# Choice 1's first tiles start inside choice 0's last pass, and the expert bias is weighed ahead of the product

## The chip, the cores and the metric

The kernel runs on one core of a Trainium2 chip. The metric is the device time of one execution in microseconds (us), here the median of several runs; smaller is better. One more execution is recorded by the hardware profiler, and every row below is from it. PE is the matrix engine (TensorE), DVE the vector engine, ACT the scalar engine, POOL is GpSimd, and SP only issues DMAs.

## What is computed

The block takes x (4 x 2048 tokens of 512 numbers), adds a gated cross attention over 77 context tokens, and then a gated mixture of experts. Only the second part matters here. It is, shortened:

```python
gate_probs = softmax(layernorm(x) @ gate_w.T + gate_b)     # 8 experts and 2 that do nothing
weights, selected = top_k(gate_probs, 2)
norm_w = weights * (selected < 8) / their_sum
out = sum over the two choices of norm_w * (y @ expert_w[e] + expert_b[e])   # y = layernorm(x)
x = x + tanh(g_ffn) * out
```

So each token goes through the expert of its choice 0 and then through that of its choice 1.

## The kernel before

**The whole.** `fold_context` prepares weights, `attend` makes the attention of all 64 tiles of 128 tokens and the routing, and `run_experts` does the experts. Each function is a block of its own, with a meeting of all engines between them. The first two take 1009 us of the 1440 and are almost untouched; the experts take the rest.

**The table.** For every token and choice `attend` writes a row (token, weight, layernorm numbers) into a table in HBM, sorted by expert, with scatters that POOL issues (`scatter`, L1544, 128 rows each). The weight already has the factor tanh(g_ffn). The last group's scatters for choice 1 are left for the start of `run_experts`. There SP fetches the slots of the table, pass by pass, once the scatters have landed.

**The tiles of the experts.** Choice 0 has 50 tiles of 128 tokens here, choice 1 has 70. They are worked off in passes of five (R = RING = 5): a first pass written out, a loop `Fori` with a conditional body for the inner passes (the longest possible count, so that some turns are skipped), and a last pass written out. The helper `run` makes these for every engine. At the start of each pass DVE and PE load the five expert numbers into registers (L1679). A tile goes this way:

1. DVE names its tokens (`name_token`, L1877); POOL gathers its rows (L1740) into a ring of five. For choice 0 a row is x alone (256 KB a tile), for choice 1 it is x and the sum so far, as choice 0 left it (512 KB).
2. ACT normalizes it to y (L1845); PE transposes y (L1799); ACT makes the high half of the transposed y (`high_y`, L1837), DVE the low half (`low_y`, L1890).
3. PE multiplies (`multiply`, L1812, 12 matmuls) into one of three banks.
4. DVE's `finish`: it adds the bias to product / W_SCALE into `biased` (L1894), names the target rows (L1907 or L1910), and makes result = biased * weight + what was gathered (L1914).
5. POOL scatters the result: for choice 0 into the sum in `comb`, for choice 1 into the output (both L1761).

**What sets the order.** Every engine works through a list that is written out by hand. At step s PE has transpose s+1, then product s; DVE has low half s+1, `finish` of s, token names of s+5; POOL has the scatter of s-1, then the gather of s+4, which goes into the ring place that result s-1 has just freed. Semaphores carry all waits.

**Between the choices.** Choice 1 adds to sums which choice 0 writes, so a full gather has to wait until all scatters of choice 0 have landed. Four tiles (EARLY = 4) are therefore split: their x half is gathered during choice 0's last pass, their sum half afterwards. PE, ACT and DVE begin choice 1 only behind choice 0, ACT and DVE with a wait for all of its tiles.

## Time and profile before

| what | us |
|---|---|
| median of 3 runs | 1445.18 (1445.16 to 1447.43) |
| the profiled execution | 1441.85 |
| its span, first to last instruction | 1440.1 |
| first product of choice 0 | 1023.4 |
| first product of choice 1 | 1191.1 |
| end of the last product | 1432.3 |

PE is busy 1311.1 us of the span (91%), DVE 1139.6 (79%), ACT 794.6 (55%), POOL 694.6 (48%). A busy share over the whole says little of the last 430 us; read it by stages. [...] A timeline row has the start, the duration, the engine, the line and what is written from what; in square brackets stands how long the engine had been idle and what ended this. Buffers of `run_experts` are lent from `m_sb`, and the expert bias lies in `u_sb`, so those names stand in the rows.

### The profile page before, as it was taken

What the parts mean: (1) busy time and instruction counts of PE and PEld (TensorE: products, weight loads), DVE (VectorE), ACT (ScalarE), POOL (GpSimd) and SP (SyncE); (2) the same over time, 40 slices, a digit from 0 to 9 for tenths busy, and PEclk for the clock granted to TensorE, in tenths of its full rate; (3) what the DMA queues carried; (4) which work ended last, traced back from release to release, by engine and by line L of the source; (5) the groups of instructions that cost most, each with busy time, mean ns of one, the idle gap of its engine ahead of it and who ended that gap; (6) DMA issues with size and microseconds to landing.
All of it is one profiled execution on the core that took longest, in us unless ns stands there. A gap on an engine that the chain in (4) does not pass through costs nothing. (4 is left out here: it accounts for less than half of the span.)

```text
span 1440.1 us, 31728 instructions
## 1 busy us (share of the span) xinstructions
PE 1311.1 (91%) x7185; PEld 675.0 (47%) x7186; DVE 1139.6 (79%) x2910; ACT 794.6 (55%) x2838; POOL 694.6 (48%) x648
## 2 busy tenths in 40 slices
PE   5576699999999999999999999995699987999997
PEld 3432255555555555555555555552355543444443
DVE  5876688899999999999999999987466664666655
ACT  5775666666666666666666566661444433444432
POOL 0370123344554554454454545446566656566664
PEclk9896899999999999999999999997799998999999
DMA  5895578889897798987798987775355535677772
GB/s 195 207 270 167 171 159 198 193 208 238 222 215 188 184 225 197 252 204 191 186 233 206 247 192 188 183 167 159 95 153 152 157 126 171 201 242 223 233 224 91
DMA packets 434736, 277.64 MB, mean 193 GB/s; under 512 B 340478, under 2 KB 368190, under 8 KB 434543
## 3 DMA queue, kind: packets, MB, share of 16 engines
q1 hardware_dynamic: 406830, 202.76, 58.3%
q0 software_dynamic: 27840, 74.18, 16.3%
q8 instruction: 22, 0.36, 0.1%
q14 instruction: 44, 0.35, 0.1%
HBM read 121.27 MB, written 82.58 MB: 142 GB/s over the span
## 5 line engine op out<-in xcount | busy, mean ns | idle before, releaser
L857 PE MATMUL scores<-m_sb,zT 128*128 (+2 forms) x2304 | 415.6, 339 | 8.6 <-PEq L156 8.6
L972 ACT ACTIVATE expd<-scores,less 128x77 f32<-128x77 f32 x1024 | 317.4, 328 | 185.4 <-DVE less L1074 184.4
L872 PE MATMUL mix<-u_sb,pT 128*128 128x512 f16 x1728 | 383.5, 379 | 1.1 <-DVE x_out L1099 1.1
L1812 PE MATMUL out_bank<-w_parts,m_sb 128*128 x1440 | 338.8, 386 | 4.9 <-issue 4.1
L857 PEld LDWEIGHTS scores<-m_sb,zT 128*128 128x128 f16 x2304 | 220.8, 98 | 176.0 <-issue 12.0
L872 PEld LDWEIGHTS mix<-u_sb,pT 128*128 128x128 f16 x1728 | 169.0, 98 | 198.2 <-DVE x_out L1099 1.3
L1812 PEld LDWEIGHTS out_bank<-w_parts,m_sb 128*128 128x128 f16 x1440 | 143.2, 99 | 156.9 <-issue 19.9
L972 ACT ACTIVATION_READ_ACCUMULATOR expd<-scores,less 128x1 f32 x1024 | 213.5, 209 | 0.0
L1544 POOL DMA_INDIRECT table<-payload,row_i x128 | 158.9, 1241 | 59.5 <-issue 38.1
L1441 POOL TENSOR_TENSOR z_parts<-z,z_parts 128x512 f16<-128x512 f32 x62 | 71.7, 1156 | 193.2 <-ACT z_parts L963 193.2
L1894 DVE SCALAR_TENSOR_TENSOR m_sb<-out_bank,u_sb 128x512 f32<-128x512 f32 x120 | 82.8, 690 | 97.8 <-PE out_bank L1812 97.6
L1837 ACT CAST m_sb<-yT_bank 128x512 f16<-128x512 f32 x120 | 70.2, 585 | 153.1 <-PE yT_bank L1799 153.1
L1446 POOL TENSOR_TENSOR x_moments<-x_spread,minus_half 128x1 f32<-128x1 f32 x64 | 65.3, 1021 | 132.3 <-DVE x_spread L1109 132.3
L1890 DVE TENSOR_TENSOR m_sb<-yT_bank,m_sb 128x512 f16<-128x512 f32 x120 | 82.0, 684 | 44.8 <-issue 22.9
L1072 DVE TENSOR_REDUCE top<-scores 128x5 f32<-128x385 f32 (+1 forms) x192 | 111.1, 579 | 4.8 <-PE scores L857 4.7
L1799 PE MATMUL yT_bank<-ident,m_sb 128*128 128x128 f32 x480 | 76.6, 284 | 40.9 <-ACT m_sb L1845 36.9
L1761 POOL DMA_INDIRECT out_dram<-m_sb,token_out x70 | 72.7, 1038 | 76.5 <-DVE token L1877 42.2
L1845 ACT ACTIVATE m_sb<-two_ring,slots 128x512 f32<-128x512 f32 x70 | 56.9, 813 | 70.4 <-DMA two_ring<-comb,token 65.0
L1082 DVE SCALAR_TENSOR_TENSOR expd<-expd,inverse 128x1232 f32<-128x1232 f32 x64 | 92.3, 1442 | 2.2
L1799 PEld LDWEIGHTS yT_bank<-ident,m_sb 128*128 128x128 f32 x480 | 57.6, 144 | 76.1 <-ACT m_sb L1845 57.9
L1090 DVE TENSOR_TENSOR p_parts<-expd,p_parts 128x1232 f16<-128x1232 f32 x64 | 91.8, 1434 | 0.0
L1740 POOL DMA_INDIRECT two_ring<-comb,token x66 | 68.4, 1037 | 20.1 <-issue 20.1
(177 smaller groups left out, 1738.8 us busy)
## 6 DMA issues: line engine op xcount, KB each, us to landing
comb<-x_out SPq DMA_DIRECT2D x64, 512.0 KB, 3.2
x_ln<-in_x_dram SPq DMA_DIRECT2D x64, 256.0 KB
x_res<-in_x_dram SPq DMA_DIRECT2D x64, 256.0 KB, 2.8
w_raw<-in_L_ffn_expert_w_dram SPq DMA_DIRECT2D x64, 128.0 KB, 2.3
m_dram<-m_stage SPq DMA_DIRECT2D x32, 231.0 KB, 4.5
u_dram<-m_sb SPq DMA_DIRECT2D x48, 154.0 KB
m_sb<-m_dram SPq DMA_DIRECT2D x12, 616.0 KB, 4.5
u_sb<-u_dram SPq DMA_DIRECT2D x6, 1024.0 KB, 6.8
```

Source lines behind the costliest of these rows:

```text
L857: last = pe.matmul(scores[s][k][:, 0:n], zT[:, s, zp, t, :], m, start=(t == 0 and (zp, mp) == PRODUCTS[0]), stop=(t == DT - 1 and (zp, mp) ...
L872: last = pe.matmul(mix[:], pT[:, s, pp, k, :], u_sb[:, k, up, :], start=(k == 0 and (pp, up) == PRODUCTS[0]), stop=False)
L972: last = act.activation(expd[:, s, h * KEYS:(h + 1) * KEYS], scores[s][k][:, at:at + KEYS], ACT.Exp, bias=less[:, s, h:h + 1], scale=1.0 / ...
L1072: dve.tensor_reduce(top[:, s, h0:h0 + nh], bank, AX_X, ALU.max).then_inc(top_ready, 1)
L1082: dve.scalar_tensor_tensor(e, e, P_SCALE, inverse[:, s].unsqueeze(2).broadcast_to([P, HEADS, KEYS]), ALU.mult, ALU.mult).then_inc(p_ready, 1)
L1090: dve.tensor_tensor(p_parts[:, 1, 0:COLS], expd[:, s, :], p_parts[:, 0, 0:COLS], ALU.subtract).then_inc(p_lo_ready, 1)
L1544: pool.indirect_dma_start(table, bass.IndirectOffsetOnAxis(ap=self.row_i[:, side, TOP_K * t + k:TOP_K * t + k + 1], axis=0), self.payload[ ...
L1761: pool.indirect_dma_start(to, bass.IndirectOffsetOnAxis(ap=c.token_out[:, s, :], axis=0), result[:, s, :], None, bounds_check=to.shape[0] - 1,
L1799: last = pe.transpose(c.yT_bank[s][:, t, :], y[:, s, t * P:(t + 1) * P], ident[:])
L1812: last = pe.matmul(c.out_bank[s][:], yT[:, s, yp, t, :], w_parts[:, bass.ds(e, 1), t, wp, :].rearrange("p a n -> p (a n)"), start=(t == 0 ...
L1890: dve.tensor_tensor(yT[:, s, 1], c.yT_bank[s][:], yT[:, s, 0], ALU.subtract).then_inc(c.y_lo_ready, 1)
L1894: dve.scalar_tensor_tensor(biased[:, buffer(s), :], c.out_bank[buffer(s)][:], 1.0 / W_SCALE, expert_bias[:, bass.ds(e, 1), :].rearrange("p ...
```

## The change

**(a) The bias is weighed early.** `finish` is split in three. `name_out` names the target rows. `weigh_bias` (new L1922) makes weight * bias + what was gathered into `biased`, and needs no product. `finish` (new L1947) makes result = product * weight + `biased`: one instruction after the product. For this the weight carries 1 / W_SCALE (`ffn_gain`, one small DVE instruction in `fold_context`), and ACT multiplies the table of biases by W_SCALE (128 x 4096 numbers, once) at the end of `attend`. A product's bank is now free when the result is made, so PE waits for `result_ready` of two tiles before.

On DVE, an inner pass of choice 1, step 1, before:

```order
L1890 TENSOR_TENSOR m_sb<-yT_bank,m_sb 128x512 [waits expert_summed_1,y_hi_ready_1]
L1894 ISA [waits expert_summed_1]
L1894 SCALAR_TENSOR_TENSOR m_sb<-out_bank,u_sb 128x512
L1910 ISA [waits put1_1]
L1910 COPY token_out<-slots 128x1
L1914 ISA [waits biased_ready_1]
L1914 SCALAR_TENSOR_TENSOR m_sb<-m_sb,slots,two_ring 128x512
```

and in the changed kernel:

```order
L1909 TENSOR_TENSOR m_sb<-yT_bank,m_sb 128x512 [waits expert_summed_1,y_hi_ready_1]
L1940 ISA [waits put1_1]
L1940 COPY token_out<-slots 128x1
L1917 REGISTER_ALU
L1922 ISA [waits result_ready_1]
L1922 SCALAR_TENSOR_TENSOR m_sb<-u_sb,slots,two_ring 128x512
L1947 SCALAR_TENSOR_TENSOR m_sb<-out_bank,slots,m_sb 128x512 [waits biased_ready_1,expert_summed_1]
```

The wait for the product (`expert_summed_1`) has moved from the first of two large instructions to the second; the count of large instructions is the same.

**(b) Choice 1 starts in choice 0's last pass.** `run` takes the other choice's lead-in steps (`ahead`, `behind`). PE transposes choice 1's tile 0 before the last product of choice 0, ACT normalizes tiles 0 and 1 there, DVE makes the low half of tile 0. The waits for all tiles are replaced by waits of one tile each. In choice 1's first pass DVE makes the low halves of tiles 1 to 3 before the first result, and the results are made in the steps 2 (tile 0), 3 (1 and 2) and 4 (3 and 4).

On DVE, from the last result of choice 0 to the first of choice 1, before:

```order
L1914 SCALAR_TENSOR_TENSOR m_sb<-m_sb,slots,one_ring 128x512
L1941 REGISTER_ALU [waits expert_summed_0]
L1687 TENSOR_LOAD inner_passes [waits result_ready_0]
L1687 ISA x2
L1679 TENSOR_LOAD tile_expert
L1890 TENSOR_TENSOR m_sb<-yT_bank,m_sb 128x512 [waits y_hi_ready_1]
L1877 TENSOR_SCALAR token<-slots 128x1
L1890 TENSOR_TENSOR m_sb<-yT_bank,m_sb 128x512 [waits y_hi_ready_1]
L1894 ISA [waits expert_summed_1]
L1894 SCALAR_TENSOR_TENSOR m_sb<-out_bank,u_sb 128x512
```

and now:

```order
L1947 SCALAR_TENSOR_TENSOR m_sb<-out_bank,slots,m_sb 128x512 [waits biased_ready_0,expert_summed_0]
L1691 TENSOR_LOAD inner_passes
L1691 ISA x2
L1683 TENSOR_LOAD tile_expert
L1909 TENSOR_TENSOR m_sb<-yT_bank,m_sb 128x512 [waits y_hi_ready_1,expert_summed_0]
L1909 TENSOR_TENSOR m_sb<-yT_bank,m_sb 128x512 [waits expert_summed_1,y_hi_ready_1] x2
L1933 ISA
L1940 CAST token_out<-slots 128x1 [waits put0_0]
L1920 REGISTER_ALU [waits early_sum_in0]
L1922 ISA [waits result_ready_0]
L1922 SCALAR_TENSOR_TENSOR m_sb<-u_sb,slots,two_ring 128x512
```

Tile 0's low half stands further up now, and three more stand ahead of the first wait for a gathered sum.

**(c) Five early tiles.** EARLY = R = 5: five x halves in choice 0's last pass (two of them before the last scatter), five sum halves after it, and no full gather for tile 4.

**(d) Table scatters of choice 1.** Two more of them leave `attend` for `run_experts`. On POOL, the end of `attend` and the start of `run_experts`, before:

```order
L1544 DMA table<-payload,row_i 135168x4 x6
L1544 DMA table<-payload,row_i 135168x4 [waits payload_ready,row_i_ready,placing]
L1544 DMA table<-payload,row_i 135168x4 x3
L543 UNCONDITIONAL_BRANCH
L1737 UNCONDITIONAL_BRANCH [waits barrier_Pool_Activation_PE_DVE_SP_gather]
L1544 DMA table<-payload,row_i 135168x4 x3
L1740 DMA one_ring<-comb,token 128x512 [waits cleared,token_ready_0]
L1740 DMA one_ring<-comb,token 128x512 [waits token_ready_0]
L1544 DMA table<-payload,row_i 135168x4
L1740 DMA one_ring<-comb,token 128x512 [waits token_ready_0] x2
```

and now:

```order
L1548 DMA table<-payload,row_i 135168x4 x4
L1548 DMA table<-payload,row_i 135168x4 [waits payload_ready,row_i_ready,placing]
L1548 DMA table<-payload,row_i 135168x4 x3
L545 UNCONDITIONAL_BRANCH
L1746 UNCONDITIONAL_BRANCH [waits barrier_Pool_Activation_PE_DVE_SP_gather]
L1548 DMA table<-payload,row_i 135168x4
L1749 DMA one_ring<-comb,token 128x512 [waits cleared,token_ready_0]
L1749 DMA one_ring<-comb,token 128x512 [waits token_ready_0] x3
L1548 DMA table<-payload,row_i 135168x4 x5
```

Two scatters fewer stand before the branch, and one instead of three before the first gather.

The core of the diff:

```diff
+            act.wait_ge(bias_in, 16)
+            act.mul(expert_bias[:], expert_bias[:], W_SCALE)
...
-    EARLY = 4
+    EARLY = R
...
             for s in range(R + 1):
+                if ahead is not None and s < R:
+                    ahead(0, s - R, lambda n: s - R + n >= 0, None, R * last + R)
                 step(last, s, lambda n: s + n < R, pass_experts)
+                if behind is not None and s < R:
+                    behind(0, s - R, lambda n: s - R + n >= 0, None, R * last + R)
...
                 if later(j, 2):
-                    pe.wait_ge(c.biased_ready, j - 1)
+                    pe.wait_ge(c.result_ready, 2 * (j - 1))
                 elif c.k == 1:
-                    pe.wait_ge(choices[0].biased_ready, first_tiles - 1 + j)
+                    pe.wait_ge(choices[0].result_ready, 2 * (first_tiles - 1 + j))
...
-                if c.k == 1:
-                    act.wait_ge(choices[0].yT_summed, tiles)
-                    act.wait_ge(choices[0].expert_summed, tiles)
-                    act.nop(nofuse=True)
-                tiles = run(act, c, step, 2)
+            tiles = run(act, choices[0], steps(choices[0]), 2, behind=steps(choices[1]))
+            run(act, choices[1], steps(choices[1], tiles), 0)
...
+            def weigh_bias(c, r, s, j, e, first_tiles):
+                own = slots[:, c.k, bass.ds(j, 1), 0:2].rearrange("p a b -> p (a b)")
+                if c.k == 1 and isinstance(j, int) and j < EARLY:
+                    dve.wait_ge(early_sum_in[s], 16)
+                if later(j, 2):
+                    dve.wait_ge(c.result_ready, 2 * (j - 1))
+                    dve.nop(nofuse=True)
...
+                dve.scalar_tensor_tensor(biased[:, buffer(s), :],
+                                         expert_bias[:, bass.ds(e, 1), :].rearrange("p a n -> p (a n)"), own[:, 1:2],
+                                         c.sum_got[:, s, :], ALU.mult, ALU.add).then_inc(c.biased_ready, 1)
...
+            def finish(c, r, s, j):
+                own = slots[:, c.k, bass.ds(j, 1), 1:2].rearrange("p a b -> p (a b)")
                 dve.wait_ge(c.biased_ready, j + 1)
+                dve.wait_ge(c.expert_summed, j + 1)
+                dve.nop(nofuse=True)
+                dve.scalar_tensor_tensor(result[:, s, :], c.out_bank[buffer(s)][:], own, biased[:, buffer(s), :],
+                                         ALU.mult, ALU.add).then_inc(c.result_ready, 1)
...
+                    due = {0: (), 1: (), 2: (0,), 3: (1, 2), 4: (3, 4)}[s] if first else (s,) if live(0) else ()
```

## Rows read from the trace of the kernel before

**Rows 1.** Windows: seven passes of choice 0, best pass, nine of choice 1, changeover.

```profile
1043.94:1154.75 110.81, 108.03 (x560) 57.30 (x561) 75.79 (x176) 48.30 (x71) 71.53 (x70) 1.00 0.54 154
1076.03:1091.40 15.37, 15.30 (x80) 8.25 (x81) 10.81 (x26) 6.48 (x11) 9.93 (x10) 1.00 0.58 164
1237.38:1384.65 147.27, 142.31 (x720) 72.13 (x721) 97.91 (x226) 62.74 (x90) 92.81 (x91) 1.00 0.72 228
1190.00:1194.00 4.00, 3.49 (x11) 1.45 (x12) 1.44 (x3) 1.30 (x2) 1.12 (x2) 0.64 0.17 56
```

**Rows 2.** Timeline of PE in choice 0: start, duration, engine, line.

```profile
1079.06 2.75 PE L1812 MATMUL out_bank<-w_parts,m_sb 128*128 x12
...
1082.09 2.75 PE L1812 MATMUL out_bank<-w_parts,m_sb 128*128 x12
```

**Rows 3.** Timeline in choice 1: from a result to the fourth after it.

```profile
1241.14 0.75 DVE L1914 SCALAR_TENSOR_TENSOR m_sb<-m_sb,slots,two_ring 128x512 f32<-128x512 f32 x1
...
1242.79 1.02 POOL L1761 DMA_INDIRECT out_dram<-m_sb,token_out  x1 [0.87 <-DVE token L1877]
...
1244.11 1.02 POOL L1740 DMA_INDIRECT two_ring<-comb,token  x1 [0.30 <-issue]
...
1248.88 0.81 ACT L1845 ACTIVATE m_sb<-two_ring,slots 128x512 f32<-128x512 f32 x1 [1.15 <-DMA two_ring<-comb,token]
...
1249.82 0.63 PE L1799 MATMUL yT_bank<-ident,m_sb 128*128 128x128 f32 x4
...
1250.28 2.75 PE L1812 MATMUL out_bank<-w_parts,m_sb 128*128 x12
...
1253.66 0.68 DVE L1894 SCALAR_TENSOR_TENSOR m_sb<-out_bank,u_sb 128x512 f32<-128x512 f32 x1
...
1254.49 0.75 DVE L1914 SCALAR_TENSOR_TENSOR m_sb<-m_sb,slots,two_ring 128x512 f32<-128x512 f32 x1
```

**Rows 4.** Timeline of all engines at a pass boundary in choice 0.

```profile
1073.55 0.15 DVE L1877 TENSOR_SCALAR token<-slots 128x1 int32 x1
...
1075.14 0.69 DVE L1890 TENSOR_TENSOR m_sb<-yT_bank,m_sb 128x512 f16<-128x512 f32 x1 [1.44 <-PE out_bank L1812]
1075.59 0.59 ACT L1837 CAST m_sb<-yT_bank 128x512 f16<-128x512 f32 x1 [1.15 <-PE yT_bank L1799]
...
1076.03 0.82 PE L1812 MATMUL out_bank<-w_parts,m_sb 128*128 x3 [0.48 <-issue]
```

**Rows 5.** Timeline of all engines where the experts begin.

```profile
1007.38 0.20 DVE L1582 TENSOR_SCALAR tile_at<-ahead 128x75 int32<-128x75 f32 x1
1008.29 0.97 POOL L1544 DMA_INDIRECT table<-payload,row_i  x1 [0.30 <-issue]
1011.20 2.33 ACT L1849 ACTIVATE one_ring<-ones 128x2560 f32<-128x2560 f16 x1 [13.96 <-PEq L543]
...
1014.35 0.21 DVE L1877 TENSOR_SCALAR token<-slots 128x1 int32<-128x1 f32 x2 [6.77 <-DMA slots<-table]
...
1015.72 1.05 POOL L1740 DMA_INDIRECT one_ring<-comb,token  x1 [0.30 <-issue]
```

**Rows 6.** Timeline of all engines from choice 0 to choice 1.

```profile
1189.25 1.02 POOL L1761 DMA_INDIRECT comb<-m_sb,token_out  x1 [0.31 <-DMA comb<-m_sb,token_out]
...
1193.15 1.03 POOL L1740 DMA_INDIRECT two_ring<-comb,early_sum  x1 [2.88 <-issue]
...
1199.52 0.75 DVE L1914 SCALAR_TENSOR_TENSOR m_sb<-m_sb,slots,two_ring 128x512 f32<-128x512 f32 x1
1199.79 1.38 POOL L1761 DMA_INDIRECT out_dram<-m_sb,token_out  x1 [0.30 <-issue]
...
1205.65 4.00 PE L1812 MATMUL out_bank<-w_parts,m_sb 128*128 x12
```

**Rows 7.** Timeline of DVE and POOL at the end.

```profile
1432.48 0.69 DVE L1894 SCALAR_TENSOR_TENSOR m_sb<-out_bank,u_sb 128x512 f32<-128x512 f32 x1 [1.00 <-PE out_bank L1812]
...
1433.31 0.75 DVE L1914 SCALAR_TENSOR_TENSOR m_sb<-m_sb,slots,two_ring 128x512 f32<-128x512 f32 x1
```

More of the change, by code:

```diff
@@ L1680, in experts, with run @@
                                                             skip_runtime_bounds_check_because="list_tiles clamps it")[1]
-        def run(engine, c, step, lead, uses_experts=False):
+        def run(engine, c, step, lead, uses_experts=False, ahead=None, behind=None):
             last = engine.value_load(inner_passes[0:1, c.k:c.k + 1], min_val=0, max_val=PASSES - 2) + 1
@@ L1763, in scatter @@
                                         oob_is_err=False).then_inc(c.put[s], 16)
-            for t in range(GROUP - 1):
-                listing.scatter(pool, table, 0, t, 1, 2)
+            listing.scatter(pool, table, 1, 2, 1, 2)
             pool.wait_ge(cleared, 1)
@@ L1769, in _ @@
                 gathers(choices[0], j, j)
-                if j == 1:
-                    listing.scatter(pool, table, 0, GROUP - 1, 1, 2)
+            listing.scatter(pool, table, 1, 3, 1, 2)
+            for t in range(GROUP):
+                listing.scatter(pool, table, 0, t, 1, 2)
             for c in choices:
@@ L1779, in step @@
                         gathers(c, place, j)
-                    if c.k == 0 and 0 < s <= EARLY and not live(LEAD):
-                        pool.wait_ge(early_ready, 2 * s)
-                        pool.wait_ge(cleared, R + 1)
-                        gather(choices[1].got[s - 1], two_ring[:, s - 1, 0], halves, early_x[:, s - 1, :])
+                    if c.k == 0 and 0 < s < R and not live(LEAD):
+                        for n in (s - 1,) if s < R - 1 else (s - 1, s):
+                            pool.wait_ge(early_ready, 2 * n + 2)
+                            pool.wait_ge(cleared, R + 1)
+                            gather(choices[1].got[n], two_ring[:, n, 0], halves, early_x[:, n, :])
                 tiles = run(pool, c, step, LEAD)
@@ L1936, in step @@
                             name_early(early)
-                if c.k == 1:
-                    dve.wait_ge(choices[0].expert_summed, tiles)
-                    dve.wait_ge(choices[0].result_ready, 2 * tiles)
-                    dve.nop(nofuse=True)
-                tiles = run(dve, c, step, R, uses_experts=True)
+                return step
+            tiles = run(dve, choices[0], steps(choices[0]), R, uses_experts=True, ahead=steps(choices[1]))
+            run(dve, choices[1], steps(choices[1], tiles), 0, uses_experts=True)
 def flamingo_block(nc, x, ctx_1024, g_xattn, g_ffn, L0_xattn_ln_gamma, L0_xattn_ln_beta, L0_xattn_w_q,
```

94 lines of the change are left out of this document (54 added, 40 removed).

## The prediction

> **What bounds the kernel now.** I read the page's split of time first, then the chain that ended last, then windows and timelines of the last 430 us, which are the only part that the change touches in earnest. There the unit is the tile: four transpositions and twelve matmuls. Back to back they take 3.03 us on PE (1079.06 to 1082.09) [rows 2], so a pass of five can't take less than 15.13. A pass has 80 matmuls, so the windows give the passes: choice 0 does seven (560 matmuls) in 110.81 us, 15.83 each, and its best one in 15.37; choice 1 does nine (720) in 147.27, 16.36 each [rows 1]. PE has the full clock there. So choice 0 stands 0.7 and choice 1 stands 1.2 us a pass above PE's floor, and two things hold it up.
>
> In choice 1 it is a ring of waits [rows 3]. A result ends at 1241.89; POOL begins its scatter at 1242.79 and the gather into the freed place at 1244.11; the rows are normalized from 1248.88, transposed at 1249.82, and the product queued behind that transposition runs from 1250.28 to 1253.03. It belongs to the tile four after the first. DVE then needs two large instructions in a row, and its result ends at 1254.49 + 0.75 = 1255.24. The turn takes 13.35 us for four tiles, 3.34 a tile, against PE's 3.03; windows give 3.27 on average.
>
> At a pass boundary it is DVE [rows 4]: after its last token it loads registers, and the low half begins at 1075.14, 1.44 us idle; PE's product begins at 1076.03, 3.67 us after the one before instead of 3.03.
>
> **The change part by part.**
>
> *The start.* POOL's last table scatter of the attention starts at 1008.29 and takes 0.97, to 1009.26; DVE is done at 1007.58, and ACT is in the next block at 1011.20 [rows 5]. Two scatters fewer, at a spacing of about 1.3 (0.97 and 0.30 of issue), end POOL near 1007, so DVE becomes the last and the meeting of engines is 9.26 - 7.58 = 1.7 us earlier. SP's slots and the first tokens (1014.35) move with it. The first gather was behind three scatters at 1015.72; it now waits for the token at 1012.65, plus its 0.21 and some 0.8 until POOL issues: 1013.6. I take **-2.1**, bounds 0 (something else holds the block) and -2.6. The five scatters that follow the gathers keep POOL until about 1025, when the first result isn't there yet; the fifth gather comes 2 to 3 us later than now but is needed only near 1031. SP's fetches of choice 1's slots wait for them, and need to be there at choice 0's last step of the first pass, ten us later. The scaling of the biases by ACT is 4096 numbers; ACT's fill of 2560 takes 2.33, so some 3.8 us, and ACT is idle 13.96 us there [rows 5]. Nothing for it, 3.8 if that cover were gone. The one small DVE instruction for the gain lies in the first 15 us of the kernel, where DVE waits for loads anyway; if not, it costs some 0.15, like a token name.
>
> *The result one instruction after the product.* The large ones are still low half, weighed bias, result: 0.69, 0.75 and 0.69, the last from the bank like L1894, the middle one from two tiles in SBUF like L1914 [rows 3]. On the ring, end of product to end of result is now 1255.24 - 1253.03 = 2.2 (1.5 to 1.6 where DVE is not behind); it becomes about 0.16 + 0.69 = 0.85, if the weighed bias is done by then. I count 0.8 off the turn's average of 4 x 3.27 = 13.1, which gives 12.3, or 3.07 a tile: just above PE's floor of 12.1. Does DVE have the time? From the end of one product: result to 0.85, token, low half from about 1.1 (the transposition takes 0.6 and the high half 0.59 [rows 4] before it) to 1.8, target name, weighed bias from about 2.0 to 2.8, next product's end at 3.03. It fits with 0.2 to 0.3 to spare. At the boundary the 1.44 of loads put the low half at 2.4 to 3.05 of that count, so PE waits 0.1 instead of 0.65, but the result there is some 0.7 late, which uses most of what the next tiles have over.
>
> For choice 0, with a lighter gather, I expect passes of 15.3, near its best: 8 boundaries x 0.53 = **-4.2**, bounds -2 and 8 x 0.7 = -5.6. For choice 1 I take 15.5 a pass (four tiles at 3.07 and one boundary of 3.2): 11 undisturbed passes x 0.86 = **-9.5**; bounds 11 x 0.3 = -3.3 (the gathers answer more slowly when more is asked; they already move 228 GB/s) and 11 x 1.15 = -12.7 (nothing left above the floor).
>
> *The changeover.* Now PE gets its first product of choice 1 at 1191.11, at a reduced clock (0.64 in the window, between the two levels) [rows 1]; tile 4 waits for a full gather which follows the sums, and the product before it is held until 1205.65 and takes 4.00 instead of 2.75 [rows 6]. After: the transposition and low half of tile 0 are done when choice 0 ends, so two products run from about 1188 to 1193.6 at the full clock. Then PE stops: the third product waits for result 0, which waits for a sum half. Choice 0's last scatter stays at about 1189.4, since two x gathers stand ahead of it, and so the first sum gather stays at 1193.2 and lands near 1196.7; result 0 follows at 1198.3, the third product at 1198.4, from a cold PE. Result 1 stands behind the low half of tile 4, whose transposition stands behind the third product; by the rows' durations it ends at 1206.5, and product 3 starts then. That is no better than 1205.65. The gain is later: gather 8 leaves POOL at about 1214.3 instead of 1215.7, product 7 begins near 1221 instead of 1223.3. I take **-2**, bounds +2 (one more landing or cold stretch) and -5 (the two early products kept in full). Named covers: the added waits on DVE hold the token names and low halves queued behind them, and POOL and PE wait for those.
>
> *The end.* After the last product DVE has 1432.48 to 1434.06 [rows 7]; one instruction instead leaves 0.69: **-0.9**.
>
> Sum: -2.1 - 4.2 - 9.5 - 2 - 0.9 = -18.7. The profiled execution took 1441.85 and its median over unprofiled runs is 1445.18, 3.3 more. I make the sum against 1441.85, 1423.2, and carry the difference over: 1445.18 - 18.7 = 1426.5.
>
> **Weighed against a rule.** A scatter that starts while DVE is in L1914, the instruction with two tiles in SBUF, takes 1.38 instead of 1.02 [rows 3, 6]. [...] The weighed bias is such an instruction, and it moves to the middle of the product, where POOL works too. In my count the scatter starts at 1.75 and the weighed bias at 2.0, so POOL is first. What it does if DVE is first is rival 1.
>
> **The rivals.**
>
> 1. *Choice 1 stays bound by its ring.* If each scatter or gather meets the weighed bias and takes 0.36 more (1.38 - 1.02), or landings grow by as much, the turn is 12.7, 3.17 a tile, a pass near 15.95: 11 x 0.41 = -4.5 instead of -9.5. Total 1431.5. For it: the turn and the floor are within 0.2 already. Against: the scatter and the gather of the turn took 1.02 each [rows 3].
>
> 2. *All of it.* Changeover -5, choice 0 at 15.13, choice 1 at 15.2: -2.1 - 5.6 - 12.7 - 5 - 0.9 = -26.3, 1418.9. For it: tiles at 3.03 are common in both choices. Against: the boundary loads.
>
> 3. *Slower: DVE becomes the bound.* Its five instructions stand in one queue with three waits, two of them new, and the result can't be made before the weighed bias. Their durations add up to 0.69 + 0.75 + 0.69 + 2 x 0.15 = 2.43 [rows 3, 4]. Should the gaps be over 0.84 us together, DVE's tile passes the 3.27 of choice 1, and the kernel is slower. At 3.35 a tile, 45 tiles of choice 0 gain 0.18 and 60 of choice 1 gain 0.08: +12.9 less 5 for the ends, 1453. Against: from the end of L1894 to the start of L1914, with the naming of the target and a wait between them, there are only 0.15 us now [rows 3].
>
> 4. *It does nothing in the loops.* If the scatter isn't earlier with the result, since POOL is behind anyway (0.9 lies between result and scatter [rows 3]), only start and end stay, and the changeover may cost 2: 1445.18 - 3 + 2 = 1444.
>
> **How the numbers follow.** Forecast 0.51, rival 1 0.22, rival 2 0.17, rival 3 0.05, rival 4 0.05. About 0.2% (2.9 us) is what a measurement can tell from no change. Faster: 0.90; same: 0.05 (rival 4); slower: 0.05 (rival 3). The range takes in rivals 1 and 2 and most of the bounds around them, and leaves out 3 and 4: 1418 to 1437. The prediction is 1426.5.
>
> **What would show it.** The first gather at 1013.6 and first product near 1021.3. Passes of 15.3 in choice 0 and 15.5 in choice 1, with one DVE instruction of 0.69 between a product's end and the scatter. In the changeover two warm products, an idle stretch of some 5 us, a third near 1192 on the new clock (all 6 us earlier than my figures above, which keep the old time). Rival 1 shows as 1.38 us in POOL's issues and passes near 15.95; rival 3 as DVE without idle time and PE waiting for it. The prediction is wrong if the low half at the boundary still holds PE by 0.5, or if gathers land more than 0.4 later than now.

## The result and the profile after

The changed kernel takes 1432.07 us (median of 4 runs, 1427.87 to 1434.54); the kernel before, beside it, 1445.41. The ratio is 0.990, with an interval of 0.988 to 0.993: 13 us faster, where 18.7 were forecast. Beside the experiments below, on another chip, it took 1431.44 for 1442.06 (ratio 0.992, 0.990 to 0.994).

The profiled execution took 1434.54, the longest of the four, for 1441.85 before. But DVE's last instruction on the table's payload, near the end of the attention, ends at 1004.77 instead of 1001.21, though ahead of it only small things were changed. Over the twelve traces of the experiments that moment lies between 1000.5 and 1005.8, at 1000.5 in a second trace of the changed kernel. So the table counts from that moment, since it differs from execution to execution. Marks are ends of results (the last DVE instruction of a tile). Between the first and the fifth result 12.1 us pass in both.

| stretch, us | before | after | after, again |
|---|---|---|---|
| end of the table's payload to the first result | 28.5 | 26.9 | 26.4 |
| choice 0, 5th to 45th result (8 passes) | 126.5 | 123.0 | 123.5 |
| changeover: 45th of choice 0 to 10th of choice 1 | 66.5 | 65.2 | 66.1 |
| choice 1, 10th to 55th (9 passes) | 147.2 | 146.5 | 146.5 |
| 55th to the last | 52.1 | 48.4 | 49.6 |

Windows of the changed kernel: us, busy time and instructions of PE, PEld, DVE, ACT and POOL, granted TensorE clock (1.00 is full speed), share of the DMA engines, GB/s. The first is seven passes of choice 0, the second nine of choice 1, the others the changeover; they answer to [rows 1].

```profile
1043.15:1150.97 107.82, 107.23 (x562) 57.30 (x560) 77.12 (x176) 48.27 (x70) 79.55 (x70) 1.00 0.57 159
1237.93:1384.56 146.63, 140.67 (x723) 72.38 (x721) 99.55 (x226) 62.68 (x90) 97.29 (x91) 1.00 0.73 232
...
1190.00:1197.00 7.00, 1.15 (x8) 0.60 (x5) 2.05 (x4) 1.37 (x3) 4.16 (x4) 0.81 0.35 92
1197.00:1202.00 5.00, 4.55 (x14) 1.89 (x15) 0.27 (x2) 0.00 (x0) 3.24 (x4) 0.58 0.59 193
```

Seven passes take 107.82 instead of 110.81: 15.40 each. Nine of choice 1 take 146.63 for 147.27, which is nothing. PE is busy for 140.7 of them: it waits as before.

**The turn in choice 1**, from one result to the fourth after it, as in [rows 3] (timeline: start, duration, engine, line, and in brackets the idle time ahead and what ended it):

```profile
1267.72 0.75 DVE L1947 SCALAR_TENSOR_TENSOR m_sb<-out_bank,slots,m_sb 128x512 f32<-128x512 f32 x1
...
1269.11 0.74 DVE L1922 SCALAR_TENSOR_TENSOR m_sb<-u_sb,slots,two_ring 128x512 f32<-128x512 f32 x1
1269.36 1.38 POOL L1770 DMA_INDIRECT out_dram<-m_sb,token_out  x1 [1.66 <-DVE token_out L1940]
...
1271.05 1.02 POOL L1749 DMA_INDIRECT two_ring<-comb,token  x1 [0.30 <-DVE m_sb L1947]
...
1274.82 0.74 DVE L1922 SCALAR_TENSOR_TENSOR m_sb<-u_sb,slots,two_ring 128x512 f32<-128x512 f32 x1
1275.06 1.39 POOL L1770 DMA_INDIRECT out_dram<-m_sb,token_out  x1 [0.31 <-DVE token_out L1940]
...
1276.30 0.81 ACT L1863 ACTIVATE m_sb<-two_ring,slots 128x512 f32<-128x512 f32 x1 [2.19 <-DMA two_ring<-comb,token]
...
1277.17 0.66 PE L1811 MATMUL yT_bank<-ident,m_sb 128*128 128x128 f32 x4 [1.09 <-ACT m_sb L1863]
...
1277.66 2.75 PE L1824 MATMUL out_bank<-w_parts,m_sb 128*128 x12
...
1280.51 0.75 DVE L1947 SCALAR_TENSOR_TENSOR m_sb<-out_bank,slots,m_sb 128x512 f32<-128x512 f32 x1 [0.62 <-PE out_bank L1824]
```

One DVE instruction of 0.75 (L1947, the last line) now stands between the product of the last line but one and the end of its result, as planned. But the weighed bias (L1922) starts at 1269.11, POOL's scatter 0.25 us after it, and this scatter takes 1.38 instead of 1.02. Its gather begins 2.58 after the result's end (1268.47), against 2.22 in [rows 3]. The pair at 1274.82 and 1275.06, for a later tile, is the same meeting again. And what the gather brought is there later: 5.25 us to the normalization, against 4.77. Means over 44 turns of choice 1 (a result and the gather into its place; the normalization of what was gathered; the fourth result after the first), us:

| | result's end to gather | gather to normalization | normalization to result | turn |
|---|---|---|---|---|
| before | 2.25 | 4.76 | 6.10 | 13.10 |
| after | 2.46 | 5.21 | 5.38 | 13.05 |

Of the 0.72 taken off the third part, 0.21 went back into the first and 0.45 into the second.

**The pass boundary** in choice 0 is as forecast. The low half begins at 1076.19, and PE's products 3.16 apart instead of 3.67 [rows 4]:

```profile
1074.07 2.75 PE L1824 MATMUL out_bank<-w_parts,m_sb 128*128 x12
...
1076.19 0.69 DVE L1909 TENSOR_TENSOR m_sb<-yT_bank,m_sb 128x512 f16<-128x512 f32 x1 [1.74 <-issue]
...
1077.23 2.76 PE L1824 MATMUL out_bank<-w_parts,m_sb 128*128 x12
```

**The start** [rows 5]: DVE's and POOL's last work on the table, the first tokens, the first gather, the first product:

```profile
1008.51 0.78 DVE L1581 TENSOR_TENSOR past<-past,tiles_f 128x600 f16<-128x600 f16 x1
1008.69 1.43 POOL L1548 DMA_INDIRECT table<-payload,row_i  x1 [0.30 <-issue]
...
1010.43 0.97 POOL L1548 DMA_INDIRECT table<-payload,row_i  x1 [0.31 <-issue]
1010.79 0.20 DVE L1586 TENSOR_SCALAR tile_at<-ahead 128x75 int32<-128x75 f32 x1
...
1016.52 0.21 DVE L1893 TENSOR_SCALAR token<-slots 128x1 int32<-128x1 f32 x2 [5.53 <-DMA slots<-table]
1017.59 1.05 POOL L1749 DMA_INDIRECT one_ring<-comb,token  x1 [2.66 <-DVE token L1893]
...
1025.60 5.17 PE L1824 MATMUL out_bank<-w_parts,m_sb 128*128 x12
```

Counted from the end of the payload, the first gather starts 1.7 us earlier than before (12.8 for 14.5) and the first product 1.4 earlier (20.8 for 22.2).

**The changeover** [rows 6]: the second product of choice 1, weighed bias 0, result 0, the third product, low half 4, result 1, the fourth product:

```profile
1187.95 2.76 PE L1824 MATMUL out_bank<-w_parts,m_sb 128*128 x12
...
1195.57 0.75 DVE L1922 SCALAR_TENSOR_TENSOR m_sb<-u_sb,slots,two_ring 128x512 f32<-128x512 f32 x1 [3.01 <-DMA two_ring<-comb,early_sum]
...
1196.46 0.75 DVE L1947 SCALAR_TENSOR_TENSOR m_sb<-out_bank,slots,m_sb 128x512 f32<-128x512 f32 x1
...
1197.45 4.57 PE L1824 MATMUL out_bank<-w_parts,m_sb 128*128 x12 [6.30 <-DVE m_sb L1947]
...
1203.12 0.69 DVE L1909 TENSOR_TENSOR m_sb<-yT_bank,m_sb 128x512 f16<-128x512 f32 x1 [5.85 <-ACT m_sb L1853]
...
1204.66 0.75 DVE L1947 SCALAR_TENSOR_TENSOR m_sb<-out_bank,slots,m_sb 128x512 f32<-128x512 f32 x1
...
1205.66 5.30 PE L1824 MATMUL out_bank<-w_parts,m_sb 128*128 x12 [3.20 <-DVE token_out L1940]
```

That is the picture of the prediction nearly row for row: two products at the full clock, then PE idle; the third product (4.57 us, at a clock of 0.58 in the window) waits for result 0; result 1 stands behind low half 4; the fourth product starts at 1205.66. Counted from the 45th result of choice 0 that is 39.0 us, and 40.6 in the second trace, where before it was 37.3 (1205.65): 1.7 and 3.2 later, where the forecast had about 0.9 later. All fourteen traces have just two readings of the clock, 1.00 and 0.50, and a window's figure is their mean: windows of 1 us have 0.50 from 1196 to 1201 and 1.00 at 1202 here, and the window of [rows 1] with 0.64 has 1.00 from 1190 to 1191 and 0.50 from 1192 to 1194.

**The end** [rows 7]: one large DVE instruction after the last product, then nothing.

```profile
1426.11 0.75 DVE L1947 SCALAR_TENSOR_TENSOR m_sb<-out_bank,slots,m_sb 128x512 f32<-128x512 f32 x1 [1.12 <-PE out_bank L1824]
```

### The profile page after: what moved, and what is told of

The parts are those of the page before. It is cut to its first block and busy times, and to the rows that moved or that the text cites. A ratio compares the mean times of both kernels' runs of the same rounds, so it can differ in the third digit from the quotient of the medians.

```text
span 1432.8 us, 32049 instructions
## 1 busy us (share of the span) xinstructions
PE 1308.3 (91%) x7185; PEld 676.7 (47%) x7186; DVE 1143.8 (80%) x2912; ACT 798.1 (56%) x2839; POOL 712.5 (50%) x649
## 3 DMA queue, kind: packets, MB, share of 16 engines
q0 software_dynamic: 27856, 74.18, 16.4%
## 5 line engine op out<-in xcount | busy, mean ns | idle before, releaser
L1947 DVE SCALAR_TENSOR_TENSOR m_sb<-out_bank,slots,m_sb 128x512 f32<-128x512 f32 x120 | 90.1, 750 | 62.3 <-PE out_bank L1824 59.2
L1770 POOL DMA_INDIRECT out_dram<-m_sb,token_out x70 | 76.9, 1098 | 62.7 <-DVE token_out L1940 22.6
L1811 PEld LDWEIGHTS yT_bank<-ident,m_sb 128*128 128x128 f32 x480 | 57.9, 143 | 64.5 <-ACT m_sb L1863 43.0
L1863 ACT ACTIVATE m_sb<-two_ring,slots 128x512 f32<-128x512 f32 x70 | 57.0, 814 | 52.0 <-DMA two_ring<-comb,token 49.6
L1749 POOL DMA_INDIRECT two_ring<-comb,token x65 | 68.2, 1049 | 22.5 <-issue 18.7
```

What stands on the lines that cost most here:

```text
L1770: pool.indirect_dma_start(to, bass.IndirectOffsetOnAxis(ap=c.token_out[:, s, :], axis=0), result[:, s, :], None, bounds_check=to.shape[0] - 1,
L1811: last = pe.transpose(c.yT_bank[s][:, t, :], y[:, s, t * P:(t + 1) * P], ident[:])
L1947: dve.scalar_tensor_tensor(result[:, s, :], c.out_bank[buffer(s)][:], own, biased[:, buffer(s), :], ALU.mult, ALU.add).then_inc(c.result_r ...
```

## The experiments

The question is where the 9.5 us of choice 1 went. Three theories: (A) choice 1 is bound by the latencies in its ring of waits, and POOL's issues and the landings took back what the earlier result gave; (B) it is bound by what the DMA engines carry; (C) the rest of the change disturbs it. All times beside runs of the kernel before on the same chip. The stretches are those of the first table, from one profiled execution each. "The changed kernel" without more is the whole change: 146.5 in choice 1.

| kernel | us (ratio to before, 95%) | choice 0 | changeover | choice 1 | to the last |
|---|---|---|---|---|---|
| early result alone | 1430.6 (0.990 to 0.993) | 123.1 | 64.5 | 144.0 | 49.1 |
| both instructions behind | 1437.8 (0.995 to 0.998) | 127.2 | 63.2 | 147.5 | 50.0 |
| gather first | 1420.1 (0.982 to 0.985) | 122.4 | 63.9 | 139.1 | 45.8 |
| one input | 1422.2 (0.983 to 0.988) | 121.1 | 64.5 | 139.3 | 48.1 |
| one input, padded | 1421.5 (0.984 to 0.987) | 121.1 | 66.8 | 139.0 | 48.3 |
| ACT weighs | 1421.2 (0.984 to 0.989) | 121.3 | 65.0 | 139.4 | 48.5 |
| third product freed | 1424.9 (0.986 to 0.989) | 124.3 | 58.4 | 145.8 | 49.0 |
| gather first and freed | 1413.1 (0.978 to 0.981) | 122.3 | 56.5 | 140.0 | 45.4 |
| the same, again | 1410.9 (0.977 to 0.981) | 122.4 | 56.1 | 139.2 | 45.5 |

**1. The early result alone**, on the kernel before.

```diff
+                dve.scalar_tensor_tensor(biased[...], expert_bias[...], own[:, 1:2], c.sum_got[:, s, :], ALU.mult, ALU.add)
+                dve.wait_ge(c.expert_summed, j + 1)
+                dve.scalar_tensor_tensor(result[...], c.out_bank[...], own[:, 1:2], biased[...], ALU.mult, ALU.add)
-                dve.scalar_tensor_tensor(biased[...], c.out_bank[...], 1.0 / W_SCALE, expert_bias[...], ALU.mult, ALU.add)
-                dve.scalar_tensor_tensor(result[...], biased[...], own[:, 1:2], c.sum_got[:, s, :], ALU.mult, ALU.add)
```

> The kernel before with one part of the change alone: the bias is scaled by ACT at the start and weighed on DVE while the product runs, so that one DVE instruction stands between a product and its result. Four early rows, the start, the changeover and its waits are as before. My theory after the comparison of the two traces: this part shortens choice 0's passes from 15.82 to about 15.37 (-3.6 over 8), does next to nothing for choice 1's (16.35 both), and saves 0.9 at the end: 1445.4 - 4.5 = about 1441. Rival (the forecast's own term for choice 1 is right and something else in the change ate it): choice 1's passes fall to 15.5 here, and the time is about 1431.

Measured 1430.6, ten less than the 1441 expected: choice 0 is as expected, but choice 1 is 3.2 us better (16.04 a pass), the changeover 2.0, the start 0.9, and what follows the 55th result 2 more than the 0.9 counted for the end. The time is the rival's 1431, but not by its 15.5 a pass: choice 1 keeps most of its wait with this part by itself. So (C) explains 2.5 us at most. But this part alone is worth as much as the whole change.

**2. Both large instructions behind the product again**, on the changed kernel.

```diff
-                        weigh_bias(c, r, n, j, pass_experts[n], first_tiles)
-                        finish(c, r, n, j)
+                        add_bias(c, r, n, j, pass_experts[n], first_tiles)
+                        name_out(c, r, n, j, first_tiles)
+                        finish(c, r, n, j)
-                    pe.wait_ge(c.result_ready, 2 * (j - 1))
+                    pe.wait_ge(c.biased_ready, j - 1)
```

> The changed kernel with that part undone: the weighted product and the bias are again added by two large DVE instructions after the product; the start, the fifth early row and the waits of one tile each at the changeover stay. If the parts add up: choice 0's passes back at 15.8 and choice 1's at 16.35, so about 1432.1 + 4.5 = 1436.5. If the change of order in choice 1 only works with the early result (its first results wait for one another), the changeover loses 2 to 3 more: 1439. If it comes out at or under 1433, the split of the result gives nothing at all.

Measured 1437.8, as if the parts added up (1436.5). But the changeover is 63.2 here, 3.3 under before, and the rival had it dearer. Each part by itself is worth some: 6.3 the rest of the change, 13.5 the early result, and the whole is 10.6 to 13.3. They overlap in the changeover: with both instructions behind, a bank is free once the bias is added, which needs no sum half; in the changed kernel PE waits for the result, which does. The traces show it: counted from the 45th result, the third and fourth product start at 28.1 and 35.1 here, and at 30.8 and 39.0 in the changed kernel.

**3. Gather first.** The place in the ring is free when the weighed bias has read it.

```diff
-                    pool.wait_ge(c.result_ready, 2 * (j - R) + 2)
+                    pool.wait_ge(c.biased_ready, j - R + 1)
```

with the gather ahead of the scatter in POOL's step, and its token named between weighed bias and result.

> The changed kernel, with the gather of the tile five on released by the weighed bias instead of by the result, and issued ahead of the scatter: the place in the ring is free once its sum half has been read. If choice 1's passes of 16.35 are a ring of latencies, this takes the result (0.85), the wait for POOL and the scatter (1.3) out of it: a turn of 13.05 becomes some 10.9, under PE's 12.1, so passes of 15.2 to 15.4, 11 x 1.0 = -11 and some more in choice 0: 1420 to 1422. If instead the DMA engines carry no more than they do now (768 KB a tile, some 230 GB/s), the gathers land as much later as they start earlier (4.7 us becomes 6.5 or more), the passes stay at 16.3 and the time at 1432, within 2.

Measured 1420.1, at the lower end of what was expected; seven passes of choice 0 and nine of choice 1:

```profile
1042.63:1149.85 107.22, 106.79 (x563) 57.62 (x560) 77.27 (x176) 45.47 (x70) 76.88 (x71) 1.00 0.58 162
1235.27:1374.44 139.17, 137.66 (x722) 73.92 (x720) 99.49 (x226) 58.76 (x90) 98.21 (x91) 1.00 0.78 245
```

139.17 is 15.46 a pass, a little above the 15.2 to 15.4 expected, and the DMA engines carried 245 GB/s at a share of 0.78, where the changed kernel had 232 at 0.73. (B) falls: they carry more when asked earlier. The ring is one of latencies. The mean time from gather to normalization is now 6.19, of which about 0.9 is rows that have landed and wait for their turn (0.3 in the changed kernel).

**4. One input in SBUF.** The weight is added to the sum half; the expert's bias is left out.

```diff
-                dve.scalar_tensor_tensor(biased[...], expert_bias[...], own[:, 1:2], c.sum_got[:, s, :], ALU.mult, ALU.add)
+                dve.tensor_scalar(biased[...], c.sum_got[:, s, :], own[:, 1:2], None, ALU.add)
```

> The changed kernel with the weighed bias made by a DVE instruction with one tile in SBUF as input: the weight is added to the sum half, and the expert's bias is left out, so this is not the same result. If it is that instruction's two SBUF inputs that hold POOL's issues, the scatters go back from 1.22 to 1.02 (choice 0) and from 1.10 to 1.03 (choice 1), the turn of choice 1 gets 0.1 to 0.3 shorter, its passes 15.9 to 16.2, and the time 1428 to 1431. If it is not, the scatters stay at 1.22 and 1.10 and the time at 1432. If choice 1 is bound by bytes, the scatters may shrink but its passes stay at 16.35.

Measured 1422.2, well under the 1428 to 1431 expected: choice 0 at PE's floor (15.13 a pass), choice 1 at 15.5, result to gather back at 2.25. But the instruction was also shorter, 0.48 instead of 0.74, so this didn't separate POOL's holds from DVE's time.

**5. The same, padded** with a small instruction ahead of it, DVE as busy as with the weighed bias (97.2 us in the nine passes, for 99.6).

```diff
+                dve.tensor_scalar(pad[:], c.sum_got[:, s, 0:P], own[:, 1:2], None, ALU.add)
```

> The kernel of the run before with one SBUF input, in which the DVE instruction took 0.48 instead of 0.74, with a second small one-input instruction (128 numbers a row) put ahead of it, so that DVE is busy for about as long as with the weighed bias; the expert's bias is still left out. If the gain (passes of 15.13 and 15.51, 1422.2) came from POOL's issues no longer being held by an instruction with two SBUF inputs, all of it stays: scatters 1.01 and 1.04, passes 15.13 and 15.5, 1422 within 2. If it came from DVE being free 0.26 us sooner, it goes back to 16.2 and 1430.

Measured 1421.5, all of the gain kept. DVE's busy time isn't it.

**6. ACT weighs the bias into PSUM**, DVE adds the sum half: the reference's result, and DVE instructions as long as in the changed kernel (0.69 for 0.74).

```diff
+                act.activation(bw_banks[s % 2][:], expert_bias[...], ACT.Copy, scale=own).then_inc(bw_ready[c.k], 1)
-                dve.scalar_tensor_tensor(biased[...], expert_bias[...], own[:, 1:2], c.sum_got[:, s, :], ALU.mult, ALU.add)
+                dve.tensor_tensor(biased[...], bw_banks[s % 2][:], c.sum_got[:, s, :], ALU.add)
```

> The changed kernel with the same result, in which ACT makes weight x bias into one of two free PSUM banks (behind each high half, some 0.6 to 0.7 us), and DVE adds the sum half to it: one input in PSUM and one in SBUF, so DVE is as busy as before, and the expert's bias is in. If two inputs in SBUF are what holds POOL's issues, it comes out as the runs with one SBUF input did: scatters 1.01 to 1.04, passes of 15.15 in choice 0 and 15.5 in choice 1, 1421 to 1424. If DVE's wait for ACT, ACT's longer tile (about 2.0 of 3.03 us) or its five register loads a pass hold the chain of high half and normalization, the passes stay at 15.5 and 16.3 or above: 1431 to 1440.

> The kernel in which ACT weighs the bias into PSUM, unaltered, once more. In its first run the kernel before, too, was 17 us slower than elsewhere (1461.8 for 1444), and in its trace ACT and DVE both began 1.9 us after what PE had finished, at every second tile. If those stalls belong to the kernel (ACT's third instruction a tile), they and the passes of some 18.7 come back and it is slower than the kernel before or equal to it. If they belong to that chip, they are gone: scatters stay at 1.00 to 1.02 in choice 0, passes fall to 15.15 to 15.3 in choice 0 and 15.5 to 15.6 in choice 1, and the time is 1421 to 1425 beside a kernel before of some 1444.

The first run fell on a chip where the kernel before, too, took 1461.8, and came out at 1463.6 (ratio 1.000 to 1.004). In its trace ACT starts up to 1.9 us after PE's transposition and DVE 2.4 after PE's product, and that at nearly every second tile of choice 0:

```profile
1118.40 2.75 PE L1828 MATMUL out_bank<-w_parts,m_sb 128*128 x12
...
1120.99 0.60 PE L1815 MATMUL yT_bank<-ident,m_sb 128*128 128x128 f32 x4
...
1121.43 2.75 PE L1828 MATMUL out_bank<-w_parts,m_sb 128*128 x12
...
1123.50 0.59 ACT L1857 CAST m_sb<-yT_bank 128x512 f16<-128x512 f32 x1 [2.99 <-remote]
1123.56 0.75 DVE L1964 SCALAR_TENSOR_TENSOR m_sb<-out_bank,slots,m_sb 128x512 f32<-128x512 f32 x1 [2.89 <-remote]
```

On another chip the same kernel took 1421.2 (before: 1441.5), and no such stall is in its trace. So they aren't the kernel's alone. What they are isn't known: no kernel without ACT's third instruction was profiled on the first chip. There follow the window of nine passes of choice 1 on the second chip, POOL's groups of instructions in it (busy us, mean ns of one, idle time), and the groups of the changed kernel in its nine passes:

```profile
1231.39:1371.30 139.91, 138.62 (x722) 72.65 (x720) 97.49 (x226) 88.71 (x135) 91.99 (x91) 1.00 0.76 243
```

```profile
L1753 POOL DMA_INDIRECT two_ring<-comb,token x46 | 47.1, 1024 | 14.0 <-issue 14.0
L1774 POOL DMA_INDIRECT out_dram<-m_sb,token_out x45 | 45.9, 1019 | 34.2 <-DVE token_out L1957 21.6 <-issue 8.5 <-DVE token L1909 4.0
```

```profile
L1770 POOL DMA_INDIRECT out_dram<-m_sb,token_out x46 | 51.7, 1125 | 37.5 <-DVE token_out L1940 13.9 <-DVE token L1893 11.9 <-issue 11.8
L1749 POOL DMA_INDIRECT two_ring<-comb,token x45 | 46.7, 1038 | 13.7 <-issue 12.2 <-DVE m_sb L1947 1.5
```

Scatters take 1.019 for 1.125, and from result to gather it is 2.24 again. Two rows of its timeline answer to the pair at 1269.11 and 1269.36 above: the scatter starts 0.24 after the DVE instruction, as there, and isn't held.

```profile
1337.97 0.69 DVE L1940 TENSOR_TENSOR m_sb<-bw_bank,two_ring 128x512 f32<-128x512 f32 x1
1338.21 1.02 POOL L1774 DMA_INDIRECT out_dram<-m_sb,token_out  x1 [0.83 <-DVE token_out L1957]
```

What decides is seen best over all scatters and gathers of the experts, by how long after the start of the nearest such DVE instruction they begin (rounded to 0.1 us). Nine traces have one with two inputs in SBUF: seven with the weighed bias, the kernel before, and the one with both instructions behind. In the three runs of experiments 6 and 7 one input is in PSUM.

| begins after, us | -0.1 | 0.0 | 0.1 | 0.2 | 0.3 | 0.4 | 0.5 | 0.6 |
|---|---|---|---|---|---|---|---|---|
| two in SBUF: issues | 102 | 140 | 28 | 152 | 120 | 61 | 30 | 37 |
| mean duration | 1.02 | 1.02 | 1.36 | 1.39 | 1.36 | 1.23 | 1.15 | 1.04 |
| one in PSUM: issues | 39 | 50 | 68 | 34 | 50 | 17 | 13 | 9 |
| mean duration | 1.01 | 1.01 | 1.02 | 1.01 | 1.02 | 1.01 | 1.03 | 1.02 |

With two in SBUF, start and duration add up to 1.61 to 1.67 from 0.2 to 0.5, so a held issue ends at the same moment, whenever it began. The column 0.1 is mixed: none that began before 0.08 was held, and 19 of its 28 took 1.48 to 1.55. From 0.085 to 0.55, 381 of 383 were held; with one in PSUM none of 122 was (1.04 at most). How the DVE instruction holds an issue, no run shows. The other way nothing is held: over 500 of these DVE instructions began while POOL was in an issue, and they took 0.74 to 0.75 in the mean, as they do alone. The 0.48 us instruction of experiments 4 and 5 holds too: four issues at 0.1 took 1.26 in the mean, three at 0.2 took 1.16. Most issues beside it just began before it or with it. So experiments 4 and 5 don't show that one input in SBUF holds nothing; their instruction was short, and met POOL's issues seldom.

**7. ACT weighs**, on the kernel of experiment 9.

> The same put on the kernel with the gathers released by the weighed bias, the third product freed and the last scatter ahead of the fifth early row (1413.1). There 1.3 us lay between result and scatter and the scatters took 1.14 to 1.18; passes were 15.29 and 15.5. If what is left above PE's 15.13 is again POOL's issues held by DVE: 15.13 and 15.2 to 15.3, so 1.3 + 14 x 0.25 = 4.8 less: 1408 to 1410. If what is left there is the boundary's loads or gathers that are late: 1412 or 1413. Slower than 1415 if ACT becomes the bound.

It was run on the first of the two chips only: 1470.6, slower than the kernel before there (ratio 1.004 to 1.007), with the same stalls. So the 1408 to 1410 is neither borne out nor refuted, and what the kernel gives elsewhere is open.

**8. The third product freed.** Tile 2 uses the third bank, and result 0 the first.

```diff
-                if later(j, 2):
+                if c.k == 1 and isinstance(j, int) and j == 2:
+                    pass
+                elif later(j, 2):
                     pe.wait_ge(c.result_ready, 2 * (j - 1))
```

> The changed kernel, in which PE's product of choice 1's third tile no longer waits for the first result: its output bank is the third, which the first tile does not use. My reading of the changeover: PE stops for about 5 us after two products, since the third waits for result 0 and so for a sum half; the rest queues behind it. With the wait gone the third product runs at once, at about 6.1 us after the first one's start, at the full clock, the fourth when result 0 is there (about 9.5 after), and the tenth result of choice 1 comes 6 to 9 us earlier: 1423 to 1426. Rival: the gathers of tiles 5 on bound it anyway (one in 2.65 us from POOL, each after its result), then it gains 2 or less: 1430.

Measured 1424.9 and a changeover of 58.4, 7 us less than the changed kernel's. Low half 1, third product, result 0, result 1, and the fourth product:

```profile
1187.34 0.69 DVE L1911 TENSOR_TENSOR m_sb<-yT_bank,m_sb 128x512 f16<-128x512 f32 x1 [1.08 <-ACT m_sb L1855]
...
1189.63 2.75 PE L1826 MATMUL out_bank<-w_parts,m_sb 128*128 x12
...
1194.71 0.75 DVE L1949 SCALAR_TENSOR_TENSOR m_sb<-out_bank,slots,m_sb 128x512 f32<-128x512 f32 x1
...
1196.97 0.75 DVE L1949 SCALAR_TENSOR_TENSOR m_sb<-out_bank,slots,m_sb 128x512 f32<-128x512 f32 x1
...
1197.97 5.30 PE L1826 MATMUL out_bank<-w_parts,m_sb 128*128 x12 [5.15 <-DVE token_out L1942]
```

The third product follows at once, 6.1 us after the first, as expected, and the low half of tile 4 no longer stands ahead of result 1. The idle time moved behind it: the fourth product starts 14.5 us after the first, not 9.5, since it waits for result 1, though its bank needs only result 0. Counted from the 45th result it starts at 32.6, which is 6.4 earlier than in the changed kernel.

**9. Gather first, freed**, and choice 0's last scatter ahead of the fifth early row.

```diff
-                        for n in (s - 1,) if s < R - 1 else (s - 1, s):
+                        for n in (s - 1,):
```

> The kernel of the run before with the gathers released by the weighed bias (1420.1), and the third product freed as in the other kernel of this set, and choice 0's last scatter ahead of the fifth early row instead of behind it, which brings the sum halves 1.3 us earlier. If both gains hold beside each other: 1420.1 - 6 - 1.3 = 1411 to 1414, with choice 1's passes at 15.4. If the gather from the weighed bias already took what the changeover gave away: 1417 or more.

> The fastest kernel so far (gathers released by the weighed bias, third product freed, last scatter ahead of the fifth early row), unaltered, beside the other on the same chip. If this is a chip on which the kernel before takes some 1444: 1411 to 1414, passes 15.3 and 15.5. If it is the chip on which the kernel before took 1462: stalls of 1.9 us of ACT and DVE behind PE here as well, where ACT has only two instructions a tile, would lay them on the chip, and 1430 or more; passes of 15.3 and 15.5 there would lay them on ACT's third instruction.

Both hold beside each other: 1413.1 and 1410.9, ratio 0.979 (0.977 to 0.981) each time. It beats both kernels, the one before by 29 and 31 us, the changed one by 18.

**10. The changed kernel again.**

> The changed kernel once more, unaltered, beside the others of this set on one chip. The kernel with the early result alone was timed at 1430.6 and the whole change at 1432.1, on different chips; its steady passes in choice 1 took 16.04 against 16.30. If the rest of the change truly gives nothing, this comes out at 1430 to 1432 and the passes at 16.3; if it was the spread between executions, passes near 16.04 and 1427 to 1429.

Measured 1431.4, with 146.5 in choice 1 once more. So the 2.5 us which it loses there against the early result alone (144.0, one trace) stand in both of its traces. Its turns are 13.05 and 13.08 for 12.84; a part of this lies between gather and normalization, and a part behind it. Why is open.

## Why the prediction was right in sum, and where not

**Start, -2.1.** The first result comes 1.6 and 2.1 us earlier. With both instructions behind the product it is 1.4, and that is the start alone; the rest is the first result's own instruction less, which I had in no term. The 1.4 is short of 2.1. The first gather is only 1.7 earlier, for two reasons. POOL's last scatters of the attention begin 0.9 behind the payload instead of 0.2, since with fewer queued POOL now has to wait for it. And two of them were held (1.42 and 1.43, one of them the row at 1008.69) beside DVE instructions with two inputs in SBUF, where before it was one. So POOL is still the last there, 0.4 behind DVE. The other 0.3 is lost between the first gather and the first product; why is open.

**Choice 0, -4.2** in 8 passes: -3.6 and -3.1. Passes of 15.37 and 15.43 for the forecast's 15.3. Right, and the boundary by its mechanism: it fell from 3.67 to 3.16, for 3.13. But here too POOL was held, 23 of 35 scatters in seven passes, which the count had not: without the hold (experiments 4 to 6) the passes are 15.13 to 15.16.

**Choice 1, -9.5: the step that failed.** Nine passes gained 0.7 us, where the term had 7.7 for them. It took 0.8 off a turn of 13.1, on the ground that the scatter starts at 1.75 and the weighed bias at 2.0, "so POOL is first". In these nine passes 18 of 45 scatters begin within the weighed bias, and 13 of them are held, up to 1.51. It happens in two ways. Where DVE is behind, token, low half and name follow the result without a gap, and the weighed bias starts 0.64 after the result's end, ahead of the scatter at 0.89 (1269.11 and 1269.36; 5 of the 13). Where DVE isn't behind, the weighed bias starts 0.91 after the result's end, and not the 1.15 of the count; a scatter that has to wait for the gather ahead of it starts at 1.16 or later (1274.82 and 1275.06; 7 of the 13). Experiments 4 to 6 show what the term would have been without it: 139.0 to 139.4 for 147.2 in nine passes, 0.87 to 0.91 a pass, for the forecast's 0.86. The mechanism of the forecast was there and rival 1's was on top of it. Rival 1 was the true case for this term, and too cheap: I priced it at 0.36 of the turn, or a landing that much longer. Both came: 0.21 until the gather, 0.45 until its rows are there. The latter is also what the prediction had named as a sign of being wrong, gathers that land more than 0.4 later. About half of the latter goes with the hold (it is 4.95 instead of 5.21 when ACT weighs); the rest may come with more being asked of the DMA engines, which isn't separated. How a held issue makes a landing longer, no run shows.

**Changeover, -2.** -1.3 and -0.4. The standstill came as told, but the gain behind it did not come from where I had put it. Counted from the 45th result, gather 8 leaves POOL 1.4 and 2.1 us later than before (48.7 and 49.4 for 47.3), not 1.4 earlier, and product 7 begins at 54.9 and 55.5 for 55.0, not 2.3 earlier. What is gained there is that product 7 takes 2.75 instead of 3.71 (PE had been idle for 3.66 ahead of its transposition before, and the clock read 0.50 from 1222 to 1225) and that its result is one instruction. What I missed is that the wait which stops PE isn't needed: experiment 8 removed it for 7 us.

**End, -0.9.** The stretch from the 55th result gained 3.6 and 2.5. With the two of the eleven passes of choice 1's term that lie in it, the forecast had 2.6 there, so it came near, but for another reason: in all traces POOL is late once near the 57th tile of choice 1, a scatter starting 2.0 to 3.4 us after its result instead of about 1. Before, the pass in which this shows took 20.3 us instead of 16.4, after 17.2 and 18.4, and that is most of the gain. What of it the shorter way from product to result saves and what is chance isn't separated. The place in the kernel before, in its timeline of POOL, with 3.49 us idle ahead of a scatter whose result had ended at 1389.16:

```profile
1388.08 1.03 POOL L1740 DMA_INDIRECT two_ring<-comb,token  x1 [0.30 <-issue]
1392.59 1.02 POOL L1761 DMA_INDIRECT out_dram<-m_sb,token_out  x1 [3.49 <-DVE token L1877]
1393.91 1.02 POOL L1740 DMA_INDIRECT two_ring<-comb,token  x1 [0.30 <-issue]
```

So 1426.5 was 5.6 too low, and that it was not further off is partly luck: choice 1's nine passes missed by 7, the other stretches by 1 to 3 together, and the spread between executions hid some of it (the stretches sum to -10.8 and -8.8, the medians say -13.3 and -10.6). That rival 1's 1431.5 is so near is luck too: by its 4.5 for choice 1 the nine passes should have gained 3.7, and they gained 0.7. Rival 2 needed both choices at or near their floor and is out. Rival 3 is out: DVE is busy 99.6 of 146.6 us. Rival 4 said that choice 1 gains nothing, which is so, but not for its reason: the result does come 0.7 sooner after the product, and what follows it comes later.

## What to carry to other kernels

When an instruction is moved off a chain, ask what other engines issue in its new place (here 13 of 45 scatters were held, up to 1.51 us for 1.02), and count its start when its engine is behind, not when it is idle. A buffer should be released by its last reader: the gather needed the weighed bias and not the result, and the third product needed neither. That was worth 11 and 7 us, together more than the whole change. And a part should be timed alone: one part of this change gave all of its gain.

## What the runs showed of the hardware

- An indirect DMA's issue on POOL is held by a DVE instruction with two inputs in SBUF (0.74 us) if it begins 0.085 to 0.55 us after that instruction's start (381 of 383; the mean falls from 1.39 at 0.2 us to 1.15 at 0.5). If it begins at the same time or before, it takes 1.02. The DVE instruction isn't held by the issue: 0.74 to 0.75 either way.
- With one of the two inputs in PSUM, an instruction of nearly the same length (0.69 us) held none of 122 issues in that range.
- POOL is late at the same place, near the 57th tile of choice 1, in every trace. In the kernel before, the issue at 1392.59 stands 128 issues behind one in choice 0 that was late too (1170.37, 1.82 us idle); so it is with the early result alone, but in the changed kernel and its variants (those of the slow chip left aside) it is 130, so the distance is no rule. What POOL does there is open.
- One of the four chips of the experiments ran the kernel before 18 to 20 us slower (1461.8, for 1441.5 to 1444.1), and the granted clock of the two kernels profiled there hardly tells it: 0.961 and 0.964, for 0.963 to 0.968 on the others.
